# Laying seven inputs out partition first, and moving Wv's load to another queue, in a one-core attention and FFN kernel

## The reference

```python
def _L0_xattn_ref(hidden_states, encoder_hidden_states, Wq, Wk, Wv, Wo, gq, gk):
    q = (hidden_states @ Wq).reshape(B, Sq, H, D)          # H = 16 heads, D = 128
    k = (encoder_hidden_states @ Wk).reshape(B, Skv, H, D)
    v = (encoder_hidden_states @ Wv).reshape(B, Skv, H, D)
    q = rmsnorm(q, gq)
    k = rmsnorm(k, gk)
    scores = jnp.einsum('bqhd,bkhd->bhqk', q, k) * scale
    attn = jax.nn.softmax(scores, axis=-1)
    out = jnp.einsum('bhqk,bkhd->bqhd', attn, v)
    return out.reshape(B, Sq, H * D) @ Wo
...
h = silu(bit_linear(x, w_gate)) * bit_linear(x, w_up)
h = rms_norm(h, ln_weight)
return bit_linear(h, w_down)
...
x = x + _L0_xattn_ref(_layernorm(x), ctx_1024, Wq, Wk, Wv, Wo, gq, gk)
x = x + _L0_ffn_ref(_layernorm(x), w_gate, w_up, w_down, ln_weight)
```

## Time and profile before the change

| | us |
|---|---|
| median of 3 runs | 486.11 |
| lowest, highest | 484.92, 486.93 |
| the profiled execution | 488.34 |
| its span in the trace | 486.5 |
| busy: DVE, ACT, PE, POOL | 431.2, 434.6, 414.7, 393.5 |
| DMA, mean over the span | 103 GB/s |

### The profile page before, as it was taken

How to read it: one execution, slowest core, us unless ns; L and a number is a source line. 1 busy time by engine, 2 the same in 40 slices (tenths; PEclk the granted TensorE clock), 3 DMA queues, 4 the chain that set the end, 5 groups by cost and what they waited for, 6 DMA issues and landing times.

```text
span 486.5 us, 14502 instructions
## 1 busy us (share of the span) xinstructions
PE 414.7 (85%) x4459; PEld 313.2 (64%) x4459; DVE 431.2 (89%) x1237; ACT 434.6 (89%) x1459; POOL 393.5 (81%) x362
## 2 busy tenths in 40 slices
PE   0239786889999999999999999998999767888985
PEld 0127574667777877777778787776887544555554
DVE  0787899889999999999999999998998766899995
ACT  2298789989999999999999999999899658899983
POOL 1007477788999999999999999999899855788883
PEclk9999987999999999999999999999999899899999
DMA  7980374355655454545546455454464730010011
GB/s 260 354 247 13 99 215 77 67 121 90 126 108 109 98 118 86 115 100 105 111 87 125 90 110 105 95 121 88 97 122 88 126 69 3 0 34 33 22 34 55
DMA packets 145326, 50.18 MB, mean 103 GB/s; under 512 B 135952, under 2 KB 143120, under 8 KB 144784
## 3 DMA queue, kind: packets, MB, share of 16 engines
q1 hardware_dynamic: 144192, 46.68, 43.2%
q10 hardware_dynamic: 1104, 3.15, 1.9%
HBM read 14.16 MB, written 2.10 MB: 33 GB/s over the span
## 4 chain that ended last, share of the span: by engine, by line
ACT 47%; issue 15%; POOL 15%; DVE 6%; PE 6%; SPq 4%; DMA 4%; ACTq 0%; POOLq 0%; DVEq 0%
ACT work L655 15%; ACT kjunk L685 8%; ACT qhl L588 6%; ACT qshl L671 5%; POOL rkq L533 5%; SPq L427 3%; ACT work L673 3%; POOL phl L541 3%; ACT ohl L692 3%; POOL work L525 3%; DMA xs<-in_x 3%; ACT stage L713 2%; ACT stage L647 2%; POOL stage L554 1%; POOL qshl L516 1%
## 5 line engine op out<-in xcount | busy, mean ns | idle before, releaser
L375 PE MATMUL KQ<-hT,wqs 128*128 (+1 forms) x1536 | 103.8, 226 | 17.7 <-DVE qhl L912 12.9
L655 ACT ACTIVATE work<-SO,nbias,rkq 128x128 f32<-128x128 f32 x256 | 115.2, 479 | 2.3 <-DVE nbias L930 2.1
L533 POOL TENSOR_TENSOR rkq<-kqe,negh 128x8 f32<-128x8 f32 x65 | 111.6, 1717 | 6.7 <-DVE kqe L920 4.6
L375 PEld LDWEIGHTS KQ<-hT,wqs 128*128 128x128 f16 x1536 | 95.5, 101 | 25.8 <-issue 16.1
L516 POOL TENSOR_TENSOR qshl<-work,qshl 128x512 f16<-128x512 f32 x64 | 74.2, 1160 | 32.1 <-ACT work L673 32.1
L375 PE MATMUL EB<-As,ohl 128*128 128x256 f16 x768 | 95.0, 274 | 0.0
L375 PEld LDWEIGHTS EB<-As,ohl 128*128 128x128 f16 x768 | 75.6, 98 | 22.7 <-issue 0.5
L541 POOL TENSOR_TENSOR phl<-work,phl 128x512 f16<-128x512 f32 x64 | 74.0, 1157 | 7.0 <-DVE phl L970 5.2
L525 POOL TENSOR_TENSOR work<-work,rinv 128x512 f32<-128x512 f32 x64 | 66.5, 1039 | 4.3 <-DVE rinv L890 4.3
L375 PEld LDWEIGHTS SO<-kT,qhl 128*128 128x128 f16 x768 | 45.3, 99 | 34.6 <-DMA kT<-khl 24.3
L375 PE MATMUL SO<-kT,qhl 128*128 128x128 f16 x768 | 54.8, 222 | 10.2 <-DMA kT<-khl 7.0
(11 more groups left out here) (153 smaller groups left out, 921.5 us busy)
## 6 DMA issues: line engine op xcount, KB each, us to landing
xs<-in_x SPq DMA_DIRECT2D x4, 512.0 KB, 8.9
wvo<-in_wo SPq DMA_DIRECT2D x1, 2048.0 KB, 24.8
out<-wqs SPq DMA_DIRECT2D x16, 128.0 KB, 1.7
raw<-in_ctxT ACTq DMA_DIRECT2D x1, 1024.0 KB, 6.0
stage<-in_wk SPq DMA_DIRECT2D x1, 1024.0 KB, 14.2
stage<-in_wq SPq DMA_DIRECT2D x1, 1024.0 KB, 17.2
stage<-in_wq ACTq DMA_DIRECT2D x1, 1024.0 KB, 12.9
kT<-khl SPq DMA_TRANSPOSE x64, 2.9
```

The source lines that it names most:

```text
L375: last = matmul(out, lhsT=left(i), rhs=right(j), start=start and n == 0, stop=stop and n == 2)
L533: pool.tensor_tensor(rkq[:, g % 4, :], kqe[:, g % 2, :], negh[:, 0:2 * HG], ALU.pow).then_inc(root_ok, 1)
L655: ins = act.activation(pe[:, s, c], SB[:, c], ACT.Exp, scale=rkq[:, (g - AT_X + 1) % 4, HG + h:HG + h + 1], bias=nbias[:, s, h:h + 1], acc ...
```

## The change

The host stores seven inputs anew, so that what one partition receives is one contiguous row: `xP` and `ctxP` with the token index first, `wvP`, `woP`, `wgP`, `wuP` and `wdP` with the row within a block of 128 first. The loads read these, with the same destinations and semaphores. Per partition a block of `x` is then one row of 4 KB, `ctx`, `wv`, `wg`, `wu` and `wd` one of 8 KB and `wo` one of 16 KB. And the load of Wv is issued by SP behind Wq lower instead of by ACT behind Wq upper. The rest of the program is as it was.

```diff
@@ SP
             def x_load(i):
                 c = slice(XB * i, XB * i + XB)
-                sp.dma_start(xs[:, c, :], x[c].rearrange("b p n -> p b n")).then_inc(x_in[i], 16)
+                sp.dma_start(xs[:, c, :], xP[:, c, :]).then_inc(x_in[i], 16)
 
             x_load(0)
             sp.dma_start(wk_f, wk).then_inc(wk_in, 16)
             sp.dma_start(wq_f[:, 1, :], wq[P:2 * P]).then_inc(wq_in[1], 16)
-            sp.dma_start(wo_f, wo.rearrange("(h d) n -> d h n", d=D)).then_inc(wvo_in[0], 16)
-            sp.dma_start(c_f, ctx.rearrange("b p n -> p b n")).then_inc(c_in, 16)
+            sp.dma_start(wvT_f, wvP).then_inc(wvo_in[1], 16)
+            sp.dma_start(wo_f, woP).then_inc(wvo_in[0], 16)
+            sp.dma_start(c_f, ctxP).then_inc(c_in, 16)
             x_load(1)
...
-                    for c, n, w in ((0, KT, wgT), (2048, KT, wuT), (4096, FJ, wdT)):
+                    for c, n, w in ((0, KT, wgP), (2048, KT, wuP), (4096, FJ, wdP)):
                         sp.dma_start(stage[:, c:c + 2048].rearrange("p (k n) -> p k n", k=n),
-                                     w.rearrange("(k p) n -> p k n", p=P)).then_inc(ffn_in, 16)
+                                     w).then_inc(ffn_in, 16)
@@ ACT
             act.dma_start(wq_f[:, 0, :], wq[0:P]).then_inc(wq_in[0], 16)
-            act.dma_start(wvT_f, wvT.rearrange("(h d) c -> d h c", d=D)).then_inc(wvo_in[1], 16)
@@ host
-        "x": np.asarray(x),
-        "ctx": ctx,
+        "xP": np.asarray(x).transpose(1, 0, 2),
+        "ctxP": ctx.transpose(1, 0, 2),
-        "wvT": np.asarray(L0_xattn_Wv).T,
-        "wo": np.asarray(L0_xattn_Wo),
+        "wvP": np.asarray(L0_xattn_Wv).T.reshape(H, D, CD).transpose(1, 0, 2),
+        "woP": np.asarray(L0_xattn_Wo).reshape(H, D, DM).transpose(1, 0, 2),
-        "wgT": np.asarray(L0_ffn_w_gate).T,
-        "wuT": np.asarray(L0_ffn_w_up).T,
-        "wdT": np.asarray(L0_ffn_w_down).T,
+        "wgP": np.asarray(L0_ffn_w_gate).T.reshape(KT, P, FF).transpose(1, 0, 2),
+        "wuP": np.asarray(L0_ffn_w_up).T.reshape(KT, P, FF).transpose(1, 0, 2),
+        "wdP": np.asarray(L0_ffn_w_down).T.reshape(FJ, P, DM).transpose(1, 0, 2),
```

More of the change, by code:

```diff
@@ L68, with build_program @@
 SLOTS = 4
-def build_program(nc, x, ctx, ctxT, wq, wk, wvT, wo, gq, gk, wgT, wuT, wdT, lnw, out):
+def build_program(nc, xP, ctxP, ctxT, wq, wk, wvP, woP, gq, gk, wgP, wuP, wdP, lnw, out):
     stack = ExitStack()
```

## The result

| | before | changed |
|---|---|---|
| median of 15 runs each, us | 486.84 | 490.55 |
| lowest, highest | 483.96, 489.03 | 486.98, 492.95 |
| ratio, 95% interval | | 1.0072 [1.0048, 1.0097] |
| profiled execution, its span | 488.34, 486.5 | 487.09, 485.3 |

The change makes the kernel 3.7 us slower. Its median, 490.55 us, lies 1 us above the stated range (483.5 to 489.6). The one profiled execution of the changed kernel is among its fastest, and that of before is among its slower ones. Single executions of either kernel differ by 5 to 6 us, so the two spans say nothing on the difference, and I compare moments inside the start, which agree to 0.2 us in the three traces of the changed kernel.

A forecast was written before the change was run, and what follows sets the result against it. The middle of the run is full and unaltered, so the first 42 us, where scales wait for Wq, decide: +1.3 (Wq upper later) - 0.2 (x earlier) = +1.1 us, giving 487.2 us on the median 486.11; range 483.5 to 489.6.

The forecast's parts named there:

- The turns: DMA queues of SP and ACT: they alternate packet by packet whatever the packet size, so short rows lose.
- Part 1: Start, SP's queue: long rows land x's first block near 7 us instead of 11.4; SP's ctx stall goes.
- Part 2: Start: Wv on SP's queue; Wq upper, behind the gains' turns, lands at 17.3 us against 15.10; final maximum +1.3 us.
- Some 6 packets of Wv: Term of Wq upper's landing: Wv packets ahead of its end, within 336 KB per DMA engine.
- spread and completion: End of Wq upper's load: slowest DMA engine about 1 us behind the average, plus 0.3 us for completion.
- Rival (b): Start, ACT's queue: 4-byte packets cost more than their turn, 2.3 us; Wq upper at 19.6, 489.5 us; chance 0.14.
- VectorE's order behind it: VectorE after Wq upper lands: gains' and layernorm work, then Wq lower without waiting; final maximum 5.3 us later, at 22.6.
- Part 3: Near 32 us: VectorE's 1.43 us wait for x's second block goes, ACT's part then binds; worth -0.2 us.
- Part 4: Loads of Wv, gk and the FFN weights: their changed landing finds no waiting engine, worth 0.
- From the start to the end: Whole kernel: the start's +1.1 us carries unchanged to the end, 487.2 us on the median of 486.11.
- (a): Start: gains don't hold ACT's queue; Wq upper lands at 12.0 us, Wq lower binds; 482.1 us; chance 0.16.
- (c): Start: Wq upper lands at 15 to 16.5 us as now; 485.5 to 486.4 us; chance 0.67 with the main case.

The follow-up runs named there:

- e1: The changed kernel with gq and gk loaded behind Wq upper and their product moved behind Wq's two maxima: 486.04 us, ratio 0.9953 to before.
- e6: The changed kernel with one load of 8-byte rows for both gains, in their old place ahead of Wq upper: 487.27 us, ratio 1.0011 to before.
- e7: The changed kernel with four gain loads, the two added ones into an unread tile, VectorE waiting for all: 499.38 us, ratio 1.0264 to before.
- e12: e8 with Wv (long rows) issued by ACT behind the gains instead of by SP behind Wq lower: 484.57 us, ratio 0.9941 to before.
- e10: e8 with the FFN weights in their old short rows: 484.56 us, ratio 0.9922 to before.
- e13: e9 with its scratch tile allocated behind all others, so no other tile moves: 490.20 us, ratio 1.0071 to before.
- e9: e8 with three unused maxima on VectorE delaying the scales, and a scratch tile among the small tiles: 494.17 us, ratio 1.0134 to before.
- e14: e8 with only an unused tile of 12 bytes per partition among the small tiles: 488.92 us, ratio 1.0064 to before.
- e15: The changed kernel a third time, no edit, on the same chip as e13: 490.13 us, ratio 1.0078 to before.
- e8: The changed kernel with one gain load, placed behind Wq upper, and the gains' product behind Wq's maxima: 483.91 us, ratio 0.9930 to before.

## Why the prediction was wrong

**In short.** I forecast 487.2 us and 490.55 was measured. Of these 3.3 us, 1.2 are from the start, where the second product of q came 2.3 us later and not 1.1: Wq upper's landing was mis-sized. 1.4 us are added behind the start, where I let the end follow one to one. And 0.7 us are no part of the change: the forecast stood on the median of 3 executions of the kernel before, 486.11, and that of 15 is 486.84. With the start's 2.3 us alone the time would have been 489.2, inside the range.

**The turns** (how the queues share the engines): right, by e1, e6 and e7. Beside Wk and Wq lower the gains' packets went one for one (136 to 137), e1 puts them behind Wq upper and e7 doubles them.

**Part 1** (x at 7 us, the stall of ctx gone): right, 7.18 us; SP had issued all its loads by 5.5 us.

**Part 2, Wq upper at 17.3 us: the step that failed, by its size.** It was 19.07. Three of its terms were off. "Some 6 packets of Wv" are 8: I let ACT's queue keep the lead that it has today, but x's long rows start SP's queue as early as ACT's (first packets of SP's queue at 1.78 us instead of 3.16, by the records of the trace; ctxT landed at 7.76 us instead of 6.74), which is 0.26 MB or 0.6 us. The rate: I took 0.43 MB/us throughout, and beside the 4-byte packets it was 0.372 and 0.350 in the two stretches from 6 to 12 us: 3 x (0.058 + 0.080) / 0.43 = 1.0 us. e1, whose gains come later, has 0.419 and 0.434 in the same stretches. The first 6 us moved 0.1 MB more than today, which gives 0.2 us back. So the corrected terms make 18.7 us. The other 0.4 us are in spread and completion, for which I had allowed 1.0 and 0.3; the 0.3 stood on no row. The queues of the changed kernel from 18 to 19 us:

```profile
q1 hardware_dynamic: 30, 0.49, 114.6%
q10 hardware_dynamic: 14, 0.00, 0.8%
```

Wq upper's last 8 KB packet had ended at 17.98 us, only 0.6 us after the 17.4 of the corrected average engine. What was left in ACT's queue were its closing records, and the read came 1.09 us after that last packet. In the kernel before it is 0.63 us (14.47 to 15.10), in e1 0.70. Rival (b) had the mechanism of the second term, at 0.137 us a turn; 1.0 us for 17 turns is 0.06, close to the 0.056 that the earlier trace rows gave as the most and that I left out of the sum. The rival's landing, 19.6 us, was nearer than mine.

**VectorE's order behind it** (5.3 us from the read to the final maximum): 24.22 - 19.07 = 5.15; right. Wq lower was no longer waited for, as I said. The idle time ahead of the first read is 9.5 us in two pieces (4.57 for the gains, 4.94 for Wq upper), where I had some 7 in one: gk was there at 13.78 us and not near 12, which costs nothing, since Wq upper stands behind it in the same queue.

**Part 3** (x's second block no longer waited for, ACT's part late next): right. VectorE waits 0.87 us for ACT's high part instead. The scales are 2.9 us later, the second product of q 2.3: a gain of 0.6, as worked out for VectorE's low part of q. kqe, on the way to GpSimd's root, starts at 39.39 instead of 36.71, a gain of 0.2, which is what I booked.

**Part 4** (Wv and the FFN weights at 0): right as far as e12 and e10 can tell.

**From the start to the end.** I let the end follow the start one to one. The start gives 2.2 to 2.9 us, the time 3.5 to 3.8 by the ratios of three comparisons (1.0072, 1.0074, 1.0078). e13 shows that late scales alone bring as much; it doesn't show how. A straight line through all kernels with tiles in place (all but e7, e9 and e14) has 1.1 us of time (by the ratios; 1.0 by the medians) for 1 us of delay of the second product, with kernels up to 1.3 us off it; the kernel before lies 0.8 us under it (1.3 by the medians). So at least half of what is missing is that the kernel before is faster than its start would make it among the others, and why isn't known. Where in the program that last microsecond arises isn't settled. Between 120 and 335 us the steps of e15, e13 and e8 are the same, 20.15 us for four; single executions differ ahead of that and behind it by more than what is sought, and the intervals reach down to 2.3 us, so that a part of it may be noise.

**Rivals.** (a), the gains not holding the queue, is refuted by the packet counts. The Trainium skill's sentence ("DMA: Bandwidth & Descriptors", Queues, rings and completion order) that an engine drains a packet of typically 9 to 17 descriptors before it switches doesn't hold for rows of 4 bytes here: e6 leaves out the 8 rows of one gain vector on each engine and reads Wq upper 3.7 us earlier. Were they one turn, beside one or two packets of 8 KB, they could have cost 0.6 us at most. (c) didn't come. (b) came in part.

## What to carry to other kernels

Where two queues are busy, count turns, not bytes: a load of one element per partition cost its queue 8 turns per engine and one for its end, each about as long as the other queue's packet. Put such loads behind the loads that are waited for first, or join them. And longer rows on one queue are a cost to the other: before lengthening them, list what the other queue has at that time and who waits for it.

## What the hardware showed that I had not expected

An unused tile of 12 bytes per partition, allocated ahead of the tiles that the transposing DMAs read and write, made the kernel 5 us slower by the medians and 6.5 by the ratios (e14 over e8, 1.0064 against 0.9930): kT landed after 3.1 us instead of 2.9 in the median of 64 steps, and four steps took 20.3 to 20.5 us instead of 20.15. In the traces that is 2.3 us over the 40 steps up to 330 us; the rest of the difference lies ahead of them and behind. pT's landing stayed at 3.2 us. By the records of single packets between 140 and 330 us, kT's took 20.8 ns instead of 18.0 on average and pT's 21.6 instead of 21.4, and no group of compute instructions there was slower by more than 5 ns on average. So it is the transfer from khl to kT. Which of these two tiles' addresses matters, and by what rule, wasn't tried; 8 bytes shifted ahead of them (e7) gave the same landing. An experiment that adds a tile should add it last.
